# Dealing out statistics and residuals, and reordering three border tiles, in a three-pass decoder kernel

## The chip, the cores and the metric

The kernel runs on one core of a Trainium2 chip. The metric is the device time of one execution in microseconds (us). A core has five engines that run their own instruction streams and wait for each other by semaphores: TensorE (PE, matmuls), VectorE (DVE), ScalarE (ACT), GpSimd (POOL), and SyncE (SP), which starts the transfers here. Every stream is worked off in order.

## The reference, cut to what matters

x has 16 sequences of 256 tokens by 512 features. Three sublayers follow each other, each behind a layer norm and each added to x.

```
# 1 attention-like recurrence, R, K, V from time-mixed LN(x), 1024 wide
e  = exp(clip(W + K, -20, 10));  eu = exp(clip(U + K, -20, 10))
A  = shift(cumsum(e * V)) + eu * V;   B = shift(cumsum(e)) + eu
x  = x + (sigmoid(R) * A / B) @ Wo.T + bo
# 2 cross attention of LN(x) with ctx (one head as wide as the model)
s  = (Q @ K.T + side) / sqrt(32);  x = x + softmax(s) @ V @ Wo.T + bo
# 3 FFN on time-shifted LN(x), xr and xk
x  = x + sigmoid(xr @ Wr.T) * (relu(xk @ Wk.T)**2 @ Wv.T)
```

## The kernel before

Work is cut into 8 tiles of two sequences (512 tokens, four row blocks of 128 called s or SUB). Every matmul operand is split into a high and a low part, and a product is three matmuls (high·high, low·high, high·low; `three`, L80 to L82), so that a projection of one chunk is 12 matmuls of 512 columns. ACT writes most high parts; DVE or POOL subtracts to get the low ones (`..._rest`, `..._lo`). PSUM is used as eight banks: `bank[...]` for projections and turns (transposes on PE), `acc[s]` for the sublayer's output.

There are three passes over the tiles, each a block with a barrier at its end, and the result of a pass goes through memory to the next. Within a block the order of every engine's instructions is written out by hand.

**Attention pass.** `in_pairs` runs tile 0 alone, a hardware loop over the pairs (1,2), (3,4), (5,6), and tile 7 alone. A tile has eight chunks c of 128 output features, counted over tiles by g. For each chunk PE projects K, V and R (in this order), then the output of two chunks ago; in chunks 3 to 6 it also turns the next tile's normalised input. DVE's `body` (L736) does mix k, `quotient` and `refine` of the chunk before, `decayed` (L622), mix v, the two `clip`s (L628, L630), the scan, `weigh_own`, mix r, `weigh` (L646), the second scan and `denominator`. PE's V waits for weigh of the chunk before, and its K for decayed. ACT's body (L550) begins with `first_reciprocal` (L531) of the last chunk and ends with `log_d` (L526); the quotient on DVE needs both. The next tile's layer norm is made ahead: four `statistics` (L681) and an `aggregate` (L686) on DVE, `rstd_of` on POOL, four `normalise` (L474) on ACT. The previous tile's four `residual`s (L694) free its output banks.

**Cross pass.** `over_tiles(..., TAIL)` writes the first tile and the last two out alone, the others are a loop. In tile i PE makes scores, `query(i+1, c)`, `turn_probs`, `context(i, h)` and `output(i, c)` (L1137) with the turns of tile i+2 between. ACT makes `q_high`, `context_high` (L1209) of the next context, `probs_high` (L1232), `normalise(i+2)` (L1194), `pc_high` (L1236). DVE makes the low parts, POOL those of the context (`context_rest`, L1527) and rstd. In the last cross tile the FFN's first input is prepared too: `turn_ffn`, `leave_ffn`, `mix_ffn` (L1416) and its high and low parts, and PE ends with the receptance of row blocks 0 and 1.

**FFN pass.** Per tile: `receptance(i, s)`, `cap`, gate, `key(i, c)` with relu and square, the turns of tile i+1, `value`. In the first tile PE goes receptance 2 and 3, then keys with turns between them.

## Time and profile before

| | us |
|---|---|
| median of 3 runs | 1365.69 |
| their range | 1365.62 to 1366.47 |
| the profiled execution: time | 1365.3 |
| its span (first to last instruction) | 1363.3 |
| granted TensorE clock, mean | 0.997 of full speed |

Attention takes some 775 us of the span, cross attention 295, the FFN the rest. The profile is read in three steps: the busy times say which engine bounds; the waits say which stretches of that engine's idle time repeat, and who ended them; the timeline of a stretch shows each instruction with its start, its duration and, in brackets, the idle time of its engine before it with the event that ended it. PE's records overlap, since matmuls are pipelined: what a matmul costs is the distance of two starts, not its duration.

### The profile page before, as it was taken

To read this page: it belongs to the slowest core of one execution; us is meant where nothing else is said; L and a number is where in the kernel's file an instruction comes from. 1 tells how busy PE (TensorE), PEld (TensorE's weight loads), DVE (VectorE), ACT (ScalarE), POOL (GpSimd) and SP (SyncE) were. 2 spreads that over 40 slices of the span, in tenths; PEclk is the share of its full clock that TensorE was granted. 3 is DMA by queue.
4 is the path that set the end of the run, shared out by engine and by line. 5 is a ranking of instruction groups with operands and counts; after the bars stand their busy time and mean duration, and the time that the engine had idled before them with its cause. 6 is when DMAs were issued, how large, how long until landed. Compare 5 with 4: busy or idle time off the path is not lost. (4 is left out here: it accounts for less than half of the span.)

```text
span 1363.3 us, 19357 instructions
## 1 busy us (share of the span) xinstructions
PE 1324.1 (97%) x6330; PEld 1098.6 (81%) x6330; DVE 1096.6 (80%) x1782; ACT 817.8 (60%) x1555; POOL 632.7 (46%) x558
## 2 busy tenths in 40 slices
PE   6899999999999999999999989999999999999998
PEld 5777888887888888888887778888888778888886
DVE  6999999989999899999998766666554677777774
ACT  5875666666666666566556454444446366666664
POOL 4665344443443434434344554444446465555551
PEclk9999999999999999999999999999999999999999
DMA  9000101001001010010040454444442312222212
GB/s 351 10 28 5 62 32 57 7 31 62 25 6 62 31 62 0 31 62 0 32 193 1 177 224 159 154 144 148 143 162 110 123 32 93 92 92 92 93 62 93
DMA packets 54539, 113.92 MB, mean 84 GB/s; under 512 B 2768, under 2 KB 7120, under 8 KB 52560
## 3 DMA queue, kind: packets, MB, share of 16 engines
q1 hardware_dynamic: 54480, 113.22, 23.5%
q8 instruction: 26, 0.43, 0.1%
q14 instruction: 33, 0.27, 0.1%
HBM read 88.05 MB, written 25.17 MB: 83 GB/s over the span
## 5 line engine op out<-in xcount | busy, mean ns | idle before, releaser
L827 POOL TENSOR_TENSOR a_ss<-a_ss,a_eu 128x512 f32<-128x512 f32 x64 | 82.6, 1290 | 270.6 <-DVE a_ss L634 270.6
L494 ACT ACTIVATE k_or_row<-bank 128x512 f32<-128x512 f32 x192 | 114.9, 599 | 53.3 <-PE bank L82 49.2
L616 DVE SCALAR_TENSOR_TENSOR bank<-bank,k_or_row 128x510 f32<-128x510 f32 x192 | 132.1, 688 | 15.1 <-ACT k_or_row L494 10.2
L832 POOL TENSOR_TENSOR a_sv<-a_sv,a_euv 128x512 f32<-128x512 f32 x64 | 82.8, 1293 | 119.2 <-DVE a_sv L651 119.2
L514 ACT ACTIVATE bank<-bank,a_nbr 128x510 f32<-128x510 f32 x64 | 42.2, 659 | 119.3 <-DVE bank L616 119.3
L401 PE MATMUL bank<-a_wo_hi,a_y_hi 128*128 128x512 f32 x256 | 100.4, 392 | 0.0
L401 PE MATMUL bank<-a_wo_hi,a_y_lo 128*128 128x512 f32 x256 | 99.7, 389 | 0.0
L401 PE MATMUL bank<-a_wo_lo,a_y_hi 128*128 128x512 f32 x256 | 99.6, 389 | 0.0
L1532 POOL TENSOR_TENSOR b_cx_lo<-b_cx,b_cx_hi 128x512 fp32r<-128x512 f32 x32 | 40.6, 1297 | 112.8 <-ACT b_cx_hi L1214 112.8
L836 POOL TENSOR_TENSOR a_y_lo<-a_yy,a_y_hi 128x512 fp32r<-128x512 f32 x64 | 86.0, 1343 | 2.0 <-ACT a_y_hi L537 2.0
L634 DVE TENSOR_TENSOR_SCAN a_ss<-a_mask,a_ee 128x514 f32<-128x514 f32 x64 | 79.6, 1243 | 2.2
L651 DVE TENSOR_TENSOR_SCAN a_sv<-a_mask,a_ee 128x514 f32<-128x514 f32 x64 | 78.6, 1229 | 2.2
L1911 POOL TENSOR_TENSOR c_diff<-c_xt 128x512 f32<-128x512 f32 x28 | 35.5, 1267 | 80.9 <-ACT c_xt L1743 80.9
L509 ACT ACTIVATE a_ee<-a_ee,a_col 128x512 f32<-128x512 f32 x64 | 46.5, 726 | 36.6 <-DVE a_ee L622 36.6
L664 DVE TENSOR_TENSOR a_sv<-bank,a_sv 128x512 f32<-128x512 f32 x64 | 44.0, 687 | 25.8 <-ACT bank L531 25.7
L1236 ACT ACTIVATE b_pc_hi<-bank 128x512 fp32r<-128x512 f32 x32 | 19.1, 598 | 68.6 <-PE bank L82 68.6
L1916 POOL TENSOR_TENSOR c_mixed_k_lo<-c_mixed_k,c_mixed_k_hi 128x512 fp32r<-128x512 f32 x28 | 47.0, 1710 | 25.5 <-ACT c_mixed_k_hi L1749 25.5
L1326 DVE TENSOR_TENSOR b_pc_lo<-bank,b_pc_hi 128x512 fp32r<-128x512 f32 x32 | 22.1, 691 | 45.1 <-ACT b_pc_hi L1236 44.4
L1527 POOL TENSOR_TENSOR b_ct_lo<-b_ct,b_ct_hi 128x512 fp32r<-128x512 f32 x32 | 41.2, 1310 | 35.2 <-ACT b_ct_hi L1209 35.2
L401 PEld LDWEIGHTS bank<-a_wo_hi,a_y_hi 128*128 128x128 f32 x256 | 48.1, 188 | 10.4 <-issue 0.5
L401 PEld LDWEIGHTS bank<-a_wo_lo,a_y_hi 128*128 128x128 f32 x256 | 48.0, 188 | 10.4 <-issue 0.5
L401 PEld LDWEIGHTS bank<-a_wo_hi,a_y_lo 128*128 128x128 f32 x256 | 48.1, 188 | 10.0
(246 smaller groups left out, 4717.2 us busy)
## 6 DMA issues: line engine op xcount, KB each, us to landing
xres<-in_x SPq DMA_DIRECT2D x8, 1024.0 KB, 5.3
x_after_attention<-xres SPq DMA_DIRECT2D x8, 1024.0 KB, 4.3
xin<-x_after_attention SPq DMA_DIRECT2D x8, 1024.0 KB, 5.6
b_ct<-in_ctx_t SPq DMA_DIRECT2D x8, 1024.0 KB, 5.7
b_cx<-in_ctx SPq DMA_DIRECT2D x8, 1024.0 KB, 7.9
xres<-x_after_attention SPq DMA_DIRECT2D x8, 1024.0 KB, 5.5
x_after_cross<-xres SPq DMA_DIRECT2D x8, 1024.0 KB, 4.4
xin<-x_after_cross SPq DMA_DIRECT2D x8, 1024.0 KB, 5.6
```

Source lines behind the costliest of these rows:

```text
L401: last = te.matmul(acc[s][:, :], a[:, c % 2, t], b[:, c, :], start=(c == 0 and a is y_hi and b is wo_hi), stop=(c == HC - 1 and a is y_lo))
L494: sc.activation(u3[:, :, 1:], ps[m][:, :, :], ACT.Copy, scale=MIX[m]).then_inc(left[m], 1)
L509: sc.activation(ee3[:, :, 1:], ee3[:, :, 1:], ACT.Exp, bias=col[:, 1, c:c + 1]).then_inc(e_exp, 1)
L514: sc.activation(ps["r"][:, :, 0:T - 1], ps["r"][:, :, 0:T - 1], ACT.Exp, bias=nbr[:, c:c + 1], scale=-1.0).then_inc(r_exp, 1)
L616: ve.scalar_tensor_tensor(out=ps[m][:, :, 0:T - 1], in0=ps[m][:, :, 1:T], scalar=1.0 - MIX[m], in1=u3[:, :, 0:T - 1], op0=ALU.mult, op1=AL ...
L634: ve.tensor_tensor_scan(ss[:, :], mask_sb[:, :], ee[:, :], 0.0, ALU.mult, ALU.add).then_inc(s_scan, 1)
L651: ve.tensor_tensor_scan(sv[:, :], mask_sb[:, :], ee[:, :], 0.0, ALU.mult, ALU.add).then_inc(sv_scan, 1)
L664: ve.tensor_tensor(sv3[:, :, 0:T], work3[:, :, :], sv3[:, :, 0:T], ALU.mult).then_inc(q_done, 1)
L827: gp.tensor_tensor(ss3[:, :, 0:T], ss3[:, :, 0:T], eu[:, :, :], ALU.add).then_inc(b_done, 1)
L832: gp.tensor_tensor(sv3[:, :, 0:T], sv3[:, :, 0:T], euv[:, :, :], ALU.add).then_inc(a_done, 1)
L836: gp.tensor_tensor(y_lo[:, c % 2, :], flat(yy), y_hi[:, c % 2, :].bitcast(F32), ALU.subtract).then_inc(ylo_done, 1)
L1916: gp.tensor_tensor(m_lo[m][:, k, :], mixed_of(m, i)[:, k, :], m_hi[m][:, k, :].bitcast(F32), ALU.subtract).then_inc(mlo_done[m], 1)
```

## The change

Nothing is added or removed but positions, banks and the waits that go with them.

- Attention: DVE's statistics, aggregate and residuals, before in three bunches behind chunks 0 and 1, are dealt out over chunks 0 to 2 by a new function `between`. ACT's normalises, before a pair ahead of `exp_r` in chunks 1 and 2, are now a pair ahead of `exp_r` and a pair behind `log_d` in chunk 2. POOL's `rstd_of` goes from chunk 1 to 2.
- First cross tile: ACT does the probabilities first, then q_high(1,2), all four `context_high`, q_high(1,3), all four normalises; DVE and POOL in step.
- Last cross tile: `turn_ffn` 0 and 1 ahead of `turn_probs`, 2 and 3 behind the contexts, into the banks `acc[0]`, `acc[1]`, `bank[2]`, `bank[3]`; their leave, mix and high parts follow.
- First FFN tile: receptance(0,s) has bank s (`r_bank`); POOL's key rests come ahead of `rstd_of(1)`.

```diff
--- before.py
+++ after.py
@@ -567,9 +567,9 @@   (attention, ACT)
-                    if 1 <= c < 3 and ahead:
-                        normalise(i + 1, 2 * c - 2)
-                        normalise(i + 1, 2 * c - 1)
+                    if c == 2 and ahead:
+                        normalise(i + 1, 0)
+                        normalise(i + 1, 1)
                     exp_r(g, c)
...
                         log_d(g, 0)
+                    if c == 2 and ahead:
+                        normalise(i + 1, 2)
+                        normalise(i + 1, 3)
@@ -733,21 +736,36 @@   (attention, DVE)
+            def between(i, c):
+
+                if not is_last(i):
+                    if is_first(i) and 1 <= c < 3:
+                        statistics(1, 2 * c - 1)
+                    elif not is_first(i) and c < 2:
+                        statistics(i + 1, 2 * c)
+                    if c == 2:
+                        if is_first(i):
+                            dve.wait_ge(st_done, 2 * SUB)
+                        aggregate(i + 1)
+                if c == 2 and not is_first(i):
+                    residual(i - 1, (1,))
...
-                    if c == 1 and ahead:
+                    if c == 2 and ahead and not is_first(i):
                         dve.wait_ge(st_done, (i + 1) * SUB + SUB)
                     mix("k", g)
-                    if c == 1 and ahead:
-                        aggregate(i + 1)
+                    between(i, c)
                     if back:
                         quotient(g - 1)
                     decayed(g, c)
                     if back:
                         refine(g - 1)
+                    if c == 2 and not is_first(i):
+                        residual(i - 1, (2, 3))
                     mix("v", g)
...
-                    if c == 0 and ahead:
-                        for s in range(SUB):
-                            statistics(i + 1, s)
+                    if c < 2 and ahead:
+                        statistics(i + 1, 2 * c if is_first(i) else 2 * c + 1)
                     if c == 1 and not is_first(i):
-                        residual(i - 1, range(SUB))
+                        residual(i - 1, (0,))
@@ -856,7 +873,7 @@   (attention, POOL)
-                    if c == 1 and not is_last(i):
+                    if c == 2 and not is_last(i):
                         rstd_of(i + 1)
@@ -951,6 +968,10 @@   (cross)
+        def ffn_bank(k):
+
+            return acc[k] if k < 2 else bank[k]
@@ -1049,12 +1070,11 @@   (turn_ffn, PE)
                 if k < 2:
-                    pe.wait_ge(ptlo_done, NT * BT - 1 + k)
+                    pe.wait_ge(res_done, (NT - 1) * SUB)
                 else:
-                    pe.wait_ge(sh.k_mixed, k - 1)
+                    pe.wait_ge(ptlo_done, NT * BT - 3 + k)
@@ -1132,6 +1152,8 @@   (output, PE)
+                    if is_last(i):
+                        pe.wait_ge(sh.k_mixed, 2)
@@ -1161,6 +1183,9 @@   (body, PE)
+                else:
+                    turn_ffn(0)
+                    turn_ffn(1)
                 turn_probs(i, 0)
                 turn_probs(i, 1)
...
                 if is_last(i):
-                    turn_ffn(0)
-                    turn_ffn(1)
+                    turn_ffn(2)
+                    turn_ffn(3)
                 for c in range(KC):
-                    if is_last(i) and c in (1, 2):
-                        turn_ffn(c + 1)
                     output(i, c)
@@ -1279,8 +1302,6 @@   (body, ACT)
                     q_high(1, 1)
-                    for k in range(KC):
-                        context_high(1, k)
...
                 probs_high(i, 1)
-                if ahead:
+                if is_first(i):
+                    q_high(1, 2)
+                    for k in range(KC):
+                        context_high(1, k)
+                    q_high(1, 3)
+                    normalise(2, range(SUB))
+                elif ahead:
                     normalise(i + 2, (0, 1))
...
+                if not ahead:
+                    leave_ffn(0)
+                    leave_ffn(1)
                 for c in range(KC):
                     pc_high(i, c)
+                    if not ahead and c == 1:
+                        leave_ffn(2)
+                        leave_ffn(3)
                     if not ahead:
-                        leave_ffn(c)
-                        if c >= 2:
-                            mixed_high_ffn(c - 2)
+                        mixed_high_ffn(c)
@@ -1469,11 +1497,7 @@   (body, DVE)
                     q_rest(1, 0)
-                    statistics(2, (0, 1))
                     q_rest(1, 1)
-                    statistics(2, (2, 3))
-                    dve.wait_ge(st_done, 3 * SUB)
-                    aggregate()
...
+                if is_first(i):
+                    q_rest(1, 2)
+                    statistics(2)
+                    q_rest(1, 3)
+                    dve.wait_ge(st_done, 3 * SUB)
+                    aggregate()
...
+                if not ahead:
+                    mix_ffn(0)
+                    mix_ffn(1)
                 for c in range(KC):
+                    if not ahead and c >= 2:
+                        mixed_rest_ffn(c - 1)
                     pc_rest(i, c)
@@ -1557,7 +1591,11 @@   (body, POOL)
-                if not is_last(i):
+                if is_first(i):
+                    for k in range(KC):
+                        context_rest(1, k)
+                    rstd_of(2)
+                elif not is_last(i):
...
@@ -1626,6 +1664,10 @@   (FFN)
+        def r_bank(i, s):
+
+            return s if is_first(i) else s % 2
...
+                if isinstance(i, int) and i == 1 and k < 2:
+                    pe.wait_ge(capped, 3 + k)
...
-                if s >= 2:
+                if is_first(i):
+                    pass
+                elif s >= 2:
                     wait(pe, capped, i * SUB + s - 1)
...
+                elif is_first(i):
+                    pe.wait_ge(capped, 1 + c)
                 else:
                     wait(pe, capped, i * SUB + 3 + c)
...
-            rstd_of(1)
             for k in range(KC):
                 mixed_rest("k", 0, k)
+            rstd_of(1)
```

Three places of the engines' streams show what moved. The first is DVE in an even tile of the attention loop, from the end of chunk 1 into chunk 2: L657 (L660 after) is the denominator, L694 (L697) the residuals, L616 (L619) a mix, L664 and L665 the quotient, L622 (L625) decayed, L673 (L676) refine. Before:

```order
L657 SCALAR_TENSOR_TENSOR a_ss<-bank,a_ss 128x2x256
L694 TENSOR_TENSOR xres<-xres,bank 128x512 x4
L615 REGISTER_ALU
L616 SCALAR_TENSOR_TENSOR bank<-bank,k_or_row 128x2x255
L664 TENSOR_TENSOR a_sv<-bank,a_sv 128x2x256
L665 TENSOR_TENSOR bank<-bank,a_ss 128x512
L622 SCALAR_TENSOR_TENSOR a_ee<-a_trem,a_negw,bank 128x2x256
L673 SCALAR_TENSOR_TENSOR a_yy<-bank,a_sv 128x512
```

After:

```order
L660 SCALAR_TENSOR_TENSOR a_ss<-bank,a_ss 128x2x256
L684 BN_STATS stats<-xin 128x6
L697 TENSOR_TENSOR xres<-xres,bank 128x512
L759 ISA
L618 REGISTER_ALU
L619 SCALAR_TENSOR_TENSOR bank<-bank,k_or_row 128x2x255
L689 BN_AGGR mv<-stats 128x2 x4
L697 TENSOR_TENSOR xres<-xres,bank 128x512
L667 TENSOR_TENSOR a_sv<-bank,a_sv 128x2x256
L668 TENSOR_TENSOR bank<-bank,a_ss 128x512
L625 SCALAR_TENSOR_TENSOR a_ee<-a_trem,a_negw,bank 128x2x256
L676 SCALAR_TENSOR_TENSOR a_yy<-bank,a_sv 128x512
```

The fourth statistic and the aggregate have come in, and three of the four residuals stand inside chunk 2 (the last two follow directly behind these rows).

The second place is ACT in the first cross tile, behind q_high(1,1): L1209 (L1232 after) is context_high, L1232 (L1255) probs_high, L1194 (L1217) normalise, L1203 (L1226) q_high, L1236 (L1259) pc_high(0,0). Before:

```order
L1209 ACTIVATE b_ct_hi<-b_ct_5301 128x512 x4
L1232 ACTIVATE b_pt_hi<-bank2 128x512
L1232 ACTIVATE b_pt_hi<-bank3 128x512
L1194 ACTIVATE xin<-xin,nmr,rstd 128x512 x2
L1203 ACTIVATE b_q_hi_5303<-bank0,qb 128x512
L1194 ACTIVATE xin<-xin,nmr,rstd 128x512 x2
L1203 ACTIVATE b_q_hi_5303<-bank1,qb 128x512
L1236 ACTIVATE b_pc_hi<-bank0 128x512
```

After:

```order
L1255 ACTIVATE b_pt_hi<-bank2 128x512
L1255 ACTIVATE b_pt_hi<-bank3 128x512
L1226 ACTIVATE b_q_hi_5303<-bank0,qb 128x512
L1232 ACTIVATE b_ct_hi<-b_ct_5301 128x512 x4
L1226 ACTIVATE b_q_hi_5303<-bank1,qb 128x512
L1217 ACTIVATE xin<-xin,nmr,rstd 128x512 x4
L1259 ACTIVATE b_pc_hi<-bank0 128x512
```

The four context_high have moved behind the probabilities and one q_high, and all four normalises stand together ahead of pc_high.

The third place is POOL in the same tile: L1527 (L1561 after) is context_rest, the four rows from L1517 (L1551) the rstd chain. Before:

```order
L1527 TENSOR_TENSOR b_ct_lo<-b_ct,b_ct_hi 128x512 x2
L1517 TENSOR_TENSOR rstd<-mv,eps 128x4
L1518 TENSOR_SCALAR nmr<-mv 128x4
L1520 TENSOR_TENSOR rstd<-rstd,half 128x4
L1523 TENSOR_TENSOR nmr<-nmr,rstd 128x4
L1527 TENSOR_TENSOR b_ct_lo<-b_ct,b_ct_hi 128x512 x2
```

After:

```order
L1561 TENSOR_TENSOR b_ct_lo<-b_ct,b_ct_hi 128x512 x4
L1551 TENSOR_TENSOR rstd<-mv,eps 128x4
L1552 TENSOR_SCALAR nmr<-mv 128x4
L1554 TENSOR_TENSOR rstd<-rstd,half 128x4
L1557 TENSOR_TENSOR nmr<-nmr,rstd 128x4
```

The rstd chain, for which the normalises wait, now stands behind all four rests.

## Rows read from the trace of the kernel before

**Rows 1.** The page, first part: busy time of each engine.

```profile
PE 1324.1 (97%) x6330; PEld 1098.6 (81%) x6330; DVE 1096.6 (80%) x1782; ACT 817.8 (60%) x1555; POOL 632.7 (46%) x558
```

**Rows 2.** Waits of PE: us in total, times, longest.

```profile
PE bank L80 <- DVE a_ee L646: 6.6, 12, 1.1
```

**Rows 3.** Timeline, DVE, tile 0: start, us, engine, line, operation, operands, idle before.

```profile
35.52 0.74 DVE L622 SCALAR_TENSOR_TENSOR a_ee<-a_trem,a_negw,bank 128x512 f32<-128x512 f32 x1
...
60.38 1.52 DVE L630 TENSOR_SCALAR a_ee<-a_ee 128x512 f32<-128x512 f32 x1
```

**Rows 4.** Timeline, PE, tile 0, chunk 1's K.

```profile
36.40 0.47 PE L80 MATMUL bank<-a_xt_hi,a_wk_hi 128*128 128x512 f32 x1 [2.76 <-DVE a_ee L622]
```

**Rows 5.** Timeline, DVE, attention tile 2.

```profile
206.72 0.69 DVE L664 TENSOR_TENSOR a_sv<-bank,a_sv 128x512 f32<-128x512 f32 x1 [0.48 <-ACT bank L531]
...
215.46 2.46 DVE L681 BATCH_NORM_STATS2 stats<-xin 128x6 f32<-128x512 f32 x4
...
234.01 0.42 DVE L630 TENSOR_SCALAR a_ee<-a_ee 128x512 f32<-128x512 f32 x1
...
236.84 0.75 DVE L646 SCALAR_TENSOR_TENSOR a_ee<-bank,a_col,a_ee 128x512 f32<-128x512 f32 x1
...
240.80 0.69 DVE L664 TENSOR_TENSOR a_sv<-bank,a_sv 128x512 f32<-128x512 f32 x1 [0.76 <-ACT bank L531]
...
247.04 0.74 DVE L646 SCALAR_TENSOR_TENSOR a_ee<-bank,a_col,a_ee 128x512 f32<-128x512 f32 x1
```

**Rows 6.** Timeline, PE, attention tile 2: V of chunks 3 and 4.

```profile
237.64 0.50 PE L80 MATMUL bank<-a_xt_hi,a_wv_hi 128*128 128x512 f32 x1
...
249.15 0.39 PE L80 MATMUL bank<-a_xt_hi,a_wv_hi 128*128 128x512 f32 x1
```

**Rows 7.** Timeline, ACT, first cross tile.

```profile
804.65 2.18 ACT L1209 ACTIVATE b_ct_hi<-b_ct 128x512 fp32r<-128x512 f32 x4
...
814.42 0.60 ACT L1236 ACTIVATE b_pc_hi<-bank 128x512 fp32r<-128x512 f32 x1 [0.63 <-PE bank L82]
```

**Rows 8.** Timeline, POOL, first cross tile.

```profile
805.42 2.56 POOL L1527 TENSOR_TENSOR b_ct_lo<-b_ct,b_ct_hi 128x512 fp32r<-128x512 f32 x2 [12.62 <-ACT b_ct_hi L1209]
...
809.63 2.51 POOL L1527 TENSOR_TENSOR b_ct_lo<-b_ct,b_ct_hi 128x512 fp32r<-128x512 f32 x2
```

**Rows 9.** Timeline, PE, first cross tile.

```profile
812.73 0.36 PE L80 MATMUL bank<-b_pt_hi,b_cx_hi 128*128 128x256 f32 x1 [2.35 <-DVE b_q_lo L1334]
...
816.14 0.39 PE L1137 MATMUL bank<-b_l_hi,b_pc_hi 128*128 128x512 f32 x1
```

**Rows 10.** Timeline, PE, last cross tile.

```profile
1057.89 0.58 PE L80 MATMUL bank<-b_pt_hi,b_cx_hi 128*128 128x256 f32 x1 [1.41 <-DVE b_pt_lo L1326]
...
1063.12 0.48 PE L1137 MATMUL bank<-b_l_hi,b_pc_hi 128*128 128x512 f32 x1
...
1065.94 0.28 PE L80 MATMUL bank<-b_pt_hi,b_cx_hi 128*128 128x256 f32 x1
...
1078.99 0.50 PE L80 MATMUL bank<-c_wr_hi,c_mixed_r_hi 128*128 128x512 f32 x1 [0.24 <-DVE c_mixed_r_lo L1428]
```

**Rows 11.** Stretches: us; busy (x) PE, PEld, DVE, ACT, POOL; granted clock; DMA.

```profile
37.20:41.40 4.20, 3.78 (x10) 2.51 (x9) 4.13 (x8) 4.12 (x9) 1.28 (x1) 0.59 0.00 0
1058.00:1062.40 4.40, 4.40 (x25) 4.40 (x26) 0.69 (x1) 0.60 (x1) 4.40 (x5) 0.63 0.47 184
```

**Rows 12.** Timeline, ACT, first FFN tile.

```profile
1091.13 2.94 ACT L1736 ACTIVATE xin<-xin,nmr,rstd 128x512 f32<-128x512 f32 x4 [1.69 <-POOL nmr L1903]
```

**Rows 13.** Timeline, PE, first FFN tile.

```profile
1085.80 0.50 PE L80 MATMUL bank<-c_wr_hi,c_mixed_r_hi 128*128 128x512 f32 x1 [1.07 <-DVE c_gate L1828]
...
1092.48 0.47 PE L80 MATMUL bank<-c_mixed_k_hi,c_wk_hi 128*128 128x512 f32 x1 [0.90 <-POOL c_mixed_k_lo L1916]
...
1106.89 0.48 PE L1705 MATMUL bank<-c_wv_hi,c_k_hi 128*128 128x512 f32 x1
```

**Rows 14.** Timeline, POOL, first FFN tile.

```profile
1091.06 5.01 POOL L1916 TENSOR_TENSOR c_mixed_k_lo<-c_diff,c_mixed_k_hi 128x512 fp32r<-128x512 f32 x4
```

31 lines of the change are left out of this document (13 added, 18 removed).

## The prediction

> **What bounds the kernel now.** The page's first part comes first: PE is busy for 1324.1 of a span of 1363.3 us [rows 1], so a reordering can win or lose only in PE's idle stretches. The waits of PE show the largest repeated ones [rows 2]: 12 of the attention pass for DVE's weighted V, 6.6 us in all and none above 1.1. The timelines then place these and the single ones. Each stretch that the change touches is read apart: attention tile 0, a later attention tile, the first cross tile, the last cross tile, the first FFN tile.
>
> **Part A, attention.** No instruction is added; four statistics, the aggregate, four residuals and four normalises per tile change place. DVE's order decides when PE may start the next V projection (behind weigh, L646) and K projection (behind decayed, L622).
>
> Tile 0: four statistics in a row take 2.46, as in tile 2 [rows 5], and stand ahead of chunk 1's decayed at 35.52, behind which PE waits 2.76, its longest wait in the tile [rows 3, 4]. After the change one stands behind chunk 0 and one behind mix k, so two of four, 1.2 us, leave that place, and the quotient ahead has less to wait for: decayed comes some 1.5 earlier and the wait shrinks to about 1.3. But the second pair of normalises now stands between chunk 2's logarithm and its reciprocal on ACT, 1.47 (half of four at 2.94 [rows 12]), in the chain log, reciprocal, quotient, decayed. By adding up the engine orders, chunk 2's chain ends only .15 before its old place: most of the gain is lent, and new waits of V take it back. I take −1.0; bounds 0 (all given back) and −2.8 (all of the 2.76 kept).
>
> In the same tile a clip of DVE took 1.52 [rows 3], where the same instruction takes .42 in tile 2 [rows 5]; POOL was splitting weight rows at the time. If DVE's row slides out of that coincidence, 1.1 is won there, if it slides into another it is lost; this is inside the bounds. The Trainium skill ("SBUF — State Buffer", section "Who interferes with whom") calls the port pair that VectorE and GpSimd share an exclusive lock, so that the engine which issues second stands still: by it the extra 1.1 is a matter of which of the two comes first, and tile 0 would come out at about −.15 or −1.25 instead of −1.0. The trace agrees as far as 1.52 against .42 goes, and doesn't tell which comes first after the change.
>
> Tile 1: its three late V projections lie behind the same bunch of statistics and residuals; −.5, an estimate at half of one long wait of 1.1 [rows 2].
>
> Tiles 2, 4, 6: DVE waits .48 for ACT ahead of a quotient in chunk 0 [rows 5]; one statistic (.62, a quarter of 2.46 [rows 5]) moved ahead of it fills that hole. All other moved steps still stand between this point and chunk 2's weigh. So weigh (.75 at 236.84 [rows 5]) comes about .5 earlier, some .1 of it by the wait for the input that is no longer late, and PE's V of chunk 3 (237.64 [rows 6]) is bound .3 to .4 earlier: −.4 each. What is late next is chunk 3: the pair of normalises, 1.47 less about .7 that the chain has gained ahead of it, moves the quotient at 240.80, which already waits .76 for ACT, so chunk 3's weigh (.74 at 247.04 [rows 5]) ends near 248.55, against V of chunk 4 at 249.15 − .4 = 248.75 [rows 6]. The slack is about .2, so it is hidden, barely.
>
> Tiles 3, 5 begin behind the loop's edge, where DVE starts late and has no hole to fill. The same work stands ahead of weigh; the normalise pair costs about +.1 each. Tile 7 has nothing to prepare.
>
> Sum of A: −1.0 − .5 − 1.2 + .2 = −2.5 (0 to −4.3).
>
> **Part B, first cross tile.** ACT did context_high of tile 1 (2.18 at 804.65), probabilities, normalises, and pc_high(0,0) at 814.42 [rows 7]; POOL two context rests (2.56), the rstd chain, two more (2.51 at 809.63) [rows 8]; PE waited 2.35, began context(0,0) at 812.73, and output(0,0) at 816.14 [rows 9].
> After the change the probabilities go first. PE's context(0,0) then needs no longer wait till 812.73; it starts near 810.15. But ACT's four context_high stand behind q_high(1,2), and that behind PE's query(1,2): two turns of probabilities (some .9) and 12 matmuls (2.8, as in the output of [rows 10]) behind query(1,1), which ACT had taken over before 804.65. I reckon its end at 807.6, so q_high ends at 808.2 and context_high at 810.3. POOL starts its four rests .77 behind the first of them, as it did before (805.42 against 804.65), at 808.95, and needs 2.56 + 2.51 less an overlap: 813.95. The rstd chain is now behind all four: from the end of the first pair at 807.98 to 809.63 it took 1.65, with a start lag 1.75, so 815.7. ACT's four normalises wait for it and take 2.85 (2.94 [rows 12] less overlap): 818.55. Only behind these stands pc_high(0,0): .60 and DVE's rest .75 make output(0,0) possible at 819.95. **That is 3.85 later than 816.14.** PE has done contexts (0,0) and (0,1) (1.4 each and a .7 wait between) by about 813.7, and idles some 6.2.
>
> The clock comes on top. PE fell idle for 2.76 before 36.40 [rows 4], and the stretch from 37.20 shows a granted clock of .59 over 4.20 us; after two waits of 1.41, the second of them at 1057.89 [rows 10], the stretch from 1058.00 shows .63 over 4.40 [rows 11]: 1.7 and 1.6 us lost, at the lower level of 1.2 GHz for most of each. After the 2.35 at 812.73 no fall shows. An idle of 6.2 is far beyond all three: +1.6 (0 to 2.3, the upper bound if the lower level lasts a third longer). The Trainium skill ("TensorE: Matmul & The Clock Gate", section "What's actually happening") says that the throttled state is the default and that activity releases it; by it a stretch at 1.2 GHz would surely follow this idle, and the lower bound 0 would fall away.
>
> Sum of B: +5.45 (+3.85 to +6.15).
>
> **Part C, last cross tile.** Before, PE made turns of the FFN input behind context and between the outputs. From output(0) at 1063.12 to the receptance at 1078.99 it took 15.87 [rows 10]. One output took 2.82, to 1065.94 [rows 10]; four are 11.0 where no turn slows their first matmul, and two contexts of half as many columns 2.8; the other 2.1 are two turns and waits. After: turns 0 and 1 fill the idle of 1.41 ahead of 1057.89 [rows 10], 2 and 3 follow the contexts. context(0) stays at 1057.89, since its probabilities bind. Two mix_ffn (three DVE instructions of about .69 each, the length of those in [rows 5]; 4.15) fit from 1057.75 to 1061.9, then the pc rest, and output(0) starts at 1062.7 to 1063.2 with all turns done. Plus 13.8: receptance at 1076.5 to 1077.0. **−2.2** (−2.5 at best; −1.5 if the pc rest comes one .7 step later than that).
>
> **Part D, first FFN tile.** Block entry is T = 1085.20; receptance(0,2) waited till 1085.80, key(0,0) began at 1092.48 with a wait for POOL, value at 1106.89, T + 21.69 [rows 13]. After: receptance starts at T (−.6), and POOL's four rests (5.01 [rows 14]) come first, done at T + 5.45 when key(0,0) wants them, so its four waits (2.3 in all) go. But rstd_of(1) is now behind them: T + 7.15, normalises 2.94 [rows 12], T + 10.3, and turn(1,0), which stands behind key(0,0) (T + 8.15) on PE, idles 2.2. Keys 2 and 3 wait .65 more for ACT, which is late by the normalises. Value at T + 20.9: −.8 (0 to −2.8; the latter if ACT had the normalises free in time).
>
> **Sum:** −2.5 + 5.45 − 2.2 − .8 = −.05. The profiled run had 1365.3 with a span of 1363.3; the median is 1365.69. On the median: **1365.6**, no change that a measurement can tell (it tells about 0.2%, 2.7 us, so 1363.0 to 1368.4 is "same").
>
> **Rivals.**
> *1. Faster: the new wait in the first cross tile doesn't come.* If the statistics reach POOL or the ct rests leave it sooner than I add up, pc_high isn't held and output(0,0) starts near 813.7: −2.4 in place of +5.45, so 1357.8. Against it: the orders put rstd behind four POOL rests and pc_high behind four normalises, on in-order engines. .08.
> *2. Faster: tile 0 and the FFN keep what they gain.* A to −4.0, D to −2.3: 3 us less, 1362.6. For it: the 2.76 and the four key waits are real; against: the normalise chains that follow. .16.
> *3. Slower: ACT's normalise pair, in the chain between logarithm and reciprocal.* It decides once chunk 3's chain is later than the .2 of slack. If it comes .85 later, chunk 4's V of six loop tiles starts .6 later than in the forecast: +3.6, A = +1.1, 1369.2. For it: 1.47 stands in a chain with .2 of slack; against: the earlier weigh gives part back. .12.
> *4. Slower: the dealt-out work only changes place (A = 0)*, 1368.1, and with the long clock stretch 1368.8: .10, half of it above 1368.4.
> *5. The change doesn't do what it says in the FFN:* ACT's normalises bind and D is 0: 1366.4, within "same".
> The forecast with 5 holds .54. Range 1360.5 to 1369.5: below lies rival 1, above the ends of 3 and 4. Faster .24 (1 and 2), same .54, slower .22 (3, part of 4, and sums of bounds in B).
>
> **What the profile of the changed kernel would show.** B: the gap before output(0,0) near 6 us, released by DVE's pc rest or ACT, normalises in front of pc_high, and a clock of about .6 behind it; if that gap is below 2, B is wrong. A: the wait before tile 0's second K at about 1.3, V waits of tiles 2, 4, 6 below .1 at chunk 3, and no new ones at chunk 4. C: the receptance some 13.8 behind output(0). D: no wait for the key rests, one of about 2 at turn(1,0) behind normalise. The forecast falls if loop tiles differ by over .5 each, since there are six of them.

## The result, and the profile after

The changed kernel takes 1368.97 us (median of 18 runs), the kernel before 1366.22 in the same runs (18): ratio 1.0021, 95% interval 1.0015 to 1.0027, so **2.75 us slower**. The profiled execution of the changed kernel has a span of 1365.2 against 1363.3.

Where the time went is read best from landmarks on PE, at which the work left to do is the same in both: the first matmul of a tile's last attention output, of a cross tile's first output, of the FFN's receptance, of a tile's first value. A stretch's difference is its length between two landmarks after, less before.

| stretch (up to) | before, at | after, at | difference | forecast |
|---|---|---|---|---|
| first projection | 15.60 | 15.23 | −.36 | (no part of the change) |
| attention tile 0 | 129.91 | 128.61 | −.93 | −1.0 |
| tile 1 | 221.03 | 218.98 | −.75 | −.5 |
| tiles 2, 4, 6 | | | −.12, −.19, −.33 | −.4 each |
| tiles 3, 5 | | | +.33, +.46 | +.1 each |
| tile 7, to the first scores | 789.47 | 787.58 | 0 | 0 |
| first cross output | 816.14 | 817.97 | +3.72 | +3.85 |
| second tile's output | 852.51 | 855.81 | +1.47 | +1.6 |
| last cross tile's first output | 1063.12 | 1065.97 | −.45 | −.2 |
| receptance of the FFN | 1078.99 | 1079.89 | −1.95 | −2.0 |
| first value | 1106.89 | 1108.73 | **+.94** | **−.8** |
| end | | | +.02 | 0 |

The sum is +1.86. Two lines are off: the FFN's, which has the wrong sign, and the attention loop's odd tiles. (The last cross tile's forecast of −2.2 is split here at its first output, by its own working.) A landmark stands one chunk into the next tile, since an output comes two chunks behind its projections; so an even tile's stretch includes the beginning of the odd tile behind it.

The waits of PE after (line, who ended them: us in total, times, longest):

```profile
PE bank L80 <- DVE a_ee L649: 8.8, 11, 2.0
PE bank L1159 <- DVE b_pc_lo L1354: 6.8, 2, 6.1
PE bank L1713 <- ACT xin L1784: 2.9, 1, 2.9
...
PE bank L80 <- DVE a_ee L625: 1.2, 1, 1.2
```

Against [rows 2] the attention's waits for the weighted V (L649 now) have grown from 6.6 to 8.8, and three new waits have come, one in each reordered border tile: 6.06 in the first cross tile, .73 in the last (the other of the two in the second line) and 2.88 in the first FFN tile. Tile 0's wait for decayed has shrunk from 2.76 [rows 4] to 1.2.

First cross tile, timelines of ACT, POOL and PE, and the stretch behind the first output (us, busy of PE, PEld, DVE, ACT, POOL, granted clock, DMA):

```profile
808.40 0.69 ACT L1226 ACTIVATE b_q_hi<-bank,qb 128x512 fp32r<-128x512 f32 x1
813.79 2.93 ACT L1217 ACTIVATE xin<-xin,nmr,rstd 128x512 f32<-128x512 f32 x4 [4.70 <-POOL nmr L1557]
816.62 1.05 ACT L1259 ACTIVATE b_pc_hi<-bank 128x512 fp32r<-128x512 f32 x2
```

```profile
807.02 5.04 POOL L1561 TENSOR_TENSOR b_ct_lo<-b_ct,b_ct_hi 128x512 fp32r<-128x512 f32 x4 [16.12 <-ACT b_ct_hi L1232]
812.00 0.22 POOL L1551 TENSOR_TENSOR rstd<-mv,eps 128x4 f32<-128x4 f32 x1
```

```profile
810.24 0.38 PE L80 MATMUL bank<-b_pt_hi,b_cx_hi 128*128 128x256 f32 x1 [0.46 <-DVE b_q_lo L1362]
817.97 0.79 PE L1159 MATMUL bank<-b_l_hi,b_pc_hi 128*128 128x512 f32 x1 [6.06 <-DVE b_pc_lo L1354]
```

```profile
817.90:822.00 4.10, 4.03 (x12) 3.23 (x13) 3.59 (x10) 0.00 (x0) 0.75 (x1) 0.64 0.00 0
1097.00:1101.50 4.50, 4.38 (x14) 3.64 (x15) 1.38 (x2) 4.40 (x9) 0.00 (x0) 0.62 0.00 0
```

This is the chain of the prediction, event by event: POOL's four rests to 812.0, the rstd chain, ACT's four normalises at 813.79 after 4.70 of idle, and only then both pc_high. PE waits 6.06, and the granted clock is .64 over the 4.1 us behind. In [rows 9] there was an idle of 2.35 here, and in [rows 7] pc_high stood behind two pairs of normalises that were done in time. The second line of the last fence is the FFN's: there too the granted clock is .62 over 4.5 us, and that was not in the forecast.

First FFN tile, timelines of PE, POOL and ACT:

```profile
1085.82 0.47 PE L80 MATMUL bank<-c_wr_hi,c_mixed_r_hi 128*128 128x512 f32 x1 [0.32 <-PEq L918]
...
1091.36 0.39 PE L80 MATMUL bank<-c_mixed_k_hi,c_wk_hi 128*128 128x512 f32 x1
...
1097.12 0.98 PE L1713 MATMUL bank<-ident_sb,xin 128*128 128x128 f32 x4 [2.88 <-ACT xin L1784]
```

```profile
1086.51 5.05 POOL L1964 TENSOR_TENSOR c_mixed_k_lo<-c_diff,c_mixed_k_hi 128x512 fp32r<-128x512 f32 x4 [11.41 <-ACT c_mixed_k_hi L1797]
1091.51 0.67 POOL L1945 TENSOR_TENSOR rstd<-mv,eps 128x4 f32<-128x4 f32 x1
...
1092.33 1.43 POOL L1948 TENSOR_TENSOR rstd<-rstd,half 128x4 f32<-128x4 f32 x1
```

```profile
1094.14 2.93 ACT L1784 ACTIVATE xin<-xin,nmr,rstd 128x512 f32<-128x512 f32 x4 [3.92 <-POOL nmr L1951]
```

Receptance and key start without the waits of [rows 13], as forecast: the key 5.54 behind the block's entry. But the first turn waits 2.88 for the normalises, which wait for POOL's rstd chain.

Last cross tile: one move of this part does not stand in the diff above. POOL's memset of the margin (`sh.margin`, for which every `mix_ffn` waits) stood behind POOL's twelve weight rests, and stands ahead of them now. Before, the first mix waited for it; after, it doesn't, and comes 7.9 earlier counted from the first output of the tile before (1034.26, after 1037.65). POOL and DVE before, then DVE after:

```profile
1065.44 0.10 POOL L1576 MEMSET c_xt<- 128x8 f32 x1
1065.63 0.70 DVE L1416 TENSOR_TENSOR bank<-bank,c_xt 128x512 f32<-128x512 f32 x1 [0.85 <-POOL c_xt L1576]
```

```profile
1061.14 0.69 DVE L1444 TENSOR_TENSOR bank<-bank,c_xt 128x512 f32<-128x512 f32 x1
```

The early mix of part C needs this move as much as the early turns; no run takes it out alone, so its share of the gain is open.

An even attention tile (tile 2), ACT and DVE around the end of chunk 2:

```profile
236.98 0.60 ACT L526 ACTIVATE bank<-a_ss 128x512 f32<-128x512 f32 x1 [0.53 <-DVE a_ss L660]
237.52 1.51 ACT L474 ACTIVATE xin<-xin,a_nmr,rstd 128x512 f32<-128x512 f32 x2
238.93 0.63 ACT L531 ACTIVATE bank<-bank,a_shift 128x512 f32<-128x512 f32 x1
```

```profile
239.59 0.69 DVE L667 TENSOR_TENSOR a_sv<-bank,a_sv 128x512 f32<-128x512 f32 x1 [2.05 <-ACT bank L531]
```

The pair of normalises stands between logarithm (L526) and reciprocal (L531), and DVE's quotient waits 2.05 for it, where it waited .76 [rows 5]: 1.29 lost to DVE in each of tiles 1 to 6. Whether PE feels it is the question of the experiments.

The odd tile that follows (tile 3): DVE's last residuals and PE's output of chunk 0 in chunk 2, and PE's V of chunk 3, before and after.

```profile
320.02 1.27 DVE L697 TENSOR_TENSOR xres<-xres,bank 128x512 f32<-128x512 f32 x2
```

```profile
320.30 0.39 PE L401 MATMUL bank<-a_wo_hi,a_y_lo 128*128 128x512 f32 x1
320.75 0.50 PE L401 MATMUL bank<-a_wo_hi,a_y_hi 128*128 128x512 f32 x1
```

```profile
327.73 0.50 PE L80 MATMUL bank<-a_xu_hi,a_wv_hi 128*128 128x512 f32 x1 [0.53 <-DVE a_ee L646]
325.78 0.50 PE L80 MATMUL bank<-a_xu_hi,a_wv_hi 128*128 128x512 f32 x1 [0.61 <-DVE a_ee L649]
```

The V wait was there before, and has grown by .08 only. More is lost at the output: its third bank is free when the third residual is done (the first of the pair at 320.02, which ends near 320.7), and PE starts on it .45 behind the matmul before, where the others start .23 apart. PE's lead on the kernel before shrinks by .34 there.

### The profile page after: what moved, and what is told of

The parts are those of the page before. It is cut to its first block and busy times, and to the rows that moved or that the text cites. A ratio compares the mean times of both kernels' runs of the same rounds, so it can differ in the third digit from the quotient of the medians.

```text
span 1365.2 us, 19356 instructions
## 1 busy us (share of the span) xinstructions
PE 1322.3 (97%) x6330; PEld 1098.1 (80%) x6330; DVE 1095.9 (80%) x1782; ACT 814.9 (60%) x1555; POOL 634.9 (47%) x558
## 5 line engine op out<-in xcount | busy, mean ns | idle before, releaser
L619 DVE SCALAR_TENSOR_TENSOR bank<-bank,k_or_row 128x510 f32<-128x510 f32 x192 | 132.3, 689 | 7.0 <-issue 4.0
L1259 ACT ACTIVATE b_pc_hi<-bank 128x512 fp32r<-128x512 f32 x32 | 19.0, 596 | 68.2 <-PE bank L82 68.2
L1561 POOL TENSOR_TENSOR b_ct_lo<-b_ct,b_ct_hi 128x512 fp32r<-128x512 f32 x32 | 41.1, 1308 | 38.7 <-ACT b_ct_hi L1232 38.7
L1159 PE MATMUL bank<-b_l_hi,b_pc_hi 128*128 128x512 f32 x128 | 52.5, 410 | 6.8 <-DVE b_pc_lo L1354 6.8
L526 ACT ACTIVATE bank<-a_ss 128x512 f32<-128x512 f32 x64 | 38.5, 601 | 32.4 <-DVE a_ss L660 32.4
```

The lines of the kernel that those rows point to most:

```text
L619: ve.scalar_tensor_tensor(out=ps[m][:, :, 0:T - 1], in0=ps[m][:, :, 1:T], scalar=1.0 - MIX[m], in1=u3[:, :, 0:T - 1], op0=ALU.mult, op1=AL ...
```

## The experiments

All times are medians; "against before" is the difference to the median of the kernel before in the same group of runs (1366.56 for the first four, 1366.47 for the next four, 1366.80 for the last four). The changed kernel stands at +2.75. The ratio in brackets counts all executions, also the few long ones of the last section, so in runs 5 and 8, which have several, it lies above the ratio of the medians. A difference to the changed kernel joins four medians, and by the spread of the times it is uncertain by some .9 either way; so the differences of 1.0 or less in runs 2, 5 and 11 are not clear of noise by the times alone, and are read from landmarks. These repeat well: from receptance to first value all six profiles with the FFN tile as changed have +.91 to +.94 against before, and both with the old one (runs 2 and 7) −.15. Unless it says otherwise an experiment is the changed kernel with one edit.

**1. The first cross tile put back.**

```diff
@@ (cross, ACT; DVE and POOL likewise) @@
+                    for k in range(KC):
+                        context_high(1, k)
...
-                if is_first(i):
-                    q_high(1, 2)
...
-                    normalise(2, range(SUB))
-                elif ahead:
+                if ahead:
                     normalise(i + 2, (0, 1))
```

> The changed kernel with the first cross tile put back into its old order on ScalarE, VectorE and GpSimd; everything else changed. Theory (the new wait of 6.1 us ahead of the first output, and the half clock behind it, are a loss that nothing gives back): about 5.1 less than the changed kernel, 1363.9 where that has 1369.0, so some 2.3 below the kernel before. Rival (the engines that run ahead during the wait give it back in the next cross tiles, and the loss sits in the loop tiles or the FFN): within 1 us of the changed kernel, 1368 to 1369.

Measured: 1364.24, −2.3 against before (ratio 0.9986, interval 0.9977 to 0.9995), 5.1 less than the changed kernel. The loss of this tile is real and is not given back later, and without it the kernel is faster than the one before: all other parts together gain 2.3. (In this run's profile the clock fell behind the old order's wait of 2.34, which it did not behind the 2.35 before; its first output comes .93 later than there.)

**2. The first FFN tile put back** (banks, waits, and rstd ahead of the rests).

```diff
-            return s if is_first(i) else s % 2
+            return s % 2
...
+            rstd_of(1)
             for k in range(KC):
                 mixed_rest("k", 0, k)
-            rstd_of(1)
```

> The changed kernel with the first FFN tile put back (banks, waits, and GpSimd's rstd ahead of the key rests). Theory from the two profiles (the new order of this tile loses .9: it takes away five waits of some 3.5 us, but adds one of 2.9 at the first turn and a stretch of half clock of some 1.7 behind it): .9 less than the changed kernel, 1368.1. Rival (the new order gains .8 as forecast, and the loss is elsewhere): .8 more, 1369.8.

Measured: 1368.31, +1.75 against before (1.0018, 1.0008 to 1.0029), 1.0 less than the changed kernel. The new order of this tile loses, as the profiles say and the forecast did not: by landmarks 1.1 (−.15 here, +.94 in the changed kernel).

**3. Both pairs of normalises ahead of the sigmoid exponential.**

```diff
                     if c == 2 and ahead:
-                        normalise(i + 1, 0)
-                        normalise(i + 1, 1)
+                        for s in range(SUB):
+                            normalise(i + 1, s)
...
-                    if c == 2 and ahead:
-                        normalise(i + 1, 2)
-                        normalise(i + 1, 3)
```

> The changed kernel with the second pair of normalises of the attention pass ahead of chunk 2's sigmoid exponential, together with the first, instead of between its logarithm and the reciprocal. Theory (the pair in that chain sets DVE back by 1.28 us from chunk 3 on in every tile; at the tile's end DVE is still .7 behind what PE has gained, and the odd tiles, which start from there, lose .5): the setback shrinks to some .6, the waits of PE for weigh in chunk 3 of tiles 3 and 5 from .78 to about .4, tiles 1 to 6 gain .2 to .4 each, 1367.5 (1366.8 to 1368.2) where the changed kernel has 1369.0. Rival (the odd tiles lose because the statistics stand ahead of their first quotient, behind the 2.05 of loop edge): no change, 1368.7 to 1369.3, and the waits stay at .78.

Measured: 1368.07, +1.5 against before (1.0012, 1.0003 to 1.0021), 1.25 less than the changed kernel. By landmarks, tiles 2 to 6 change from −.12, +.33, −.19, +.46, −.33 to −.43, −.30, −.47, −.06, −.45, that is 1.86 us gained, while tile 0 loses its .93: there PE now waits for the denominator of chunk 2, behind the four normalises (1.02). The odd tiles' share in the gain (.63 and .52) is there. But the waits at chunk 3 of tiles 3 and 5 shrink only from .61 and .66 to .52 and .56, and were .53 before the change, so they are not where most of the loss sat (the expectation's .78 counts the same wait from start to start). What is gone is the stop at the output of chunk 0: PE's lead on the kernel before, which shrank by .34 and .32 there in tiles 3 and 5, no longer shrinks. The loop edge is unchanged and can't be the cause by itself.

**4. The first cross tile's normalises later**, and nothing else moved.

```diff
                     q_high(1, 3)
-                    normalise(2, range(SUB))
...
                     pc_high(i, c)
+                    if is_first(i) and c == 1:
+                        normalise(2, range(SUB))
```

> The changed kernel with ScalarE's four normalises of the first cross tile behind the second high part of the context (pc_high) instead of ahead of the first; nothing else is moved. Theory (these four, which wait for GpSimd's rstd chain, are what holds the first output up): the output starts near 811.7 + 1.5 instead of 817.97 in the profile, the half clock behind it goes, and the next wait is below 1 us at the first turn of tile 2: about 6.5 less than the changed kernel, 1362.5. Rival (the rests of the context on GpSimd or VectorE's own queue hold it): the wait of 6.1 stays, or moves unshrunk to the turn, 1368 to 1369.

Measured: 1361.49, −5.1 against before (0.9964, 0.9951 to 0.9978), 7.8 less than the changed kernel. Its timeline of PE, and the stretch behind the first output:

```profile
811.87 0.38 PE L80 MATMUL bank<-b_pt_hi,b_cx_hi 128*128 128x256 f32 x1 [0.46 <-DVE b_q_lo L1363]
...
813.38 0.40 PE L1159 MATMUL bank<-b_l_hi,b_pc_hi 128*128 128x512 f32 x1
```

```profile
813.30:817.40 4.10, 4.10 (x26) 3.59 (x25) 1.68 (x4) 2.56 (x4) 3.96 (x7) 1.00 0.87 317
```

The wait of 6.06 is gone, not shrunk, and the granted clock is 1.00. The place of these four instructions alone held the tile; the rest of the tile's new order is a gain: to the first output this tile is now 2.4 shorter than before, of which .9 go again up to the next tile's output, where the first turn waits .7 for the normalises.

**5. The first FFN tile's normalises and turns put off.**

```diff
-                    if s == 1 and not is_last(i):
+                    if s == 1 and not is_last(i) and not is_first(i):
                         normalise(i + 1)
                 for c in range(KC):
                     relu_square(i, c)
+                    if is_first(i) and c == 0:
+                        normalise(1)
...
+                    if is_first(i):
+                        if c == 2:
+                            turn(1, 0)
+                        if c == 3:
+                            for k in (1, 2, 3):
+                                turn(1, k)
```

> The changed kernel with the first FFN tile's next steps put off: ScalarE makes tile 1's four normalises behind the first key's relu and square instead of ahead of gates 2 and 3, and TensorE turns tile 1's input behind keys 2 and 3 instead of one turn behind each key. Theory (the first FFN tile loses because the turn behind the first key waits 2.9 us for normalises that wait for GpSimd's rstd, now late, and the clock halves behind that wait): the wait of 2.9 and the half clock go, the remaining waits together stay near 1 us, the value begins some 18.9 behind the block's entry where the changed kernel has 22.9, that is 4 us less, 1365 where the changed kernel has 1369.0. Rival (ScalarE's whole chain of gates and relus binds this tile, so that the wait only moves to the third key): at most 1.5 less, 1367.5 to 1369.

Measured: 1368.67, +2.2 against before (1.0024, 1.0012 to 1.0036), only .55 less than the changed kernel (.87 by landmarks, up to the second tile's value). The wait of 2.88 and the low clock behind it are gone, and the value begins 20.5 behind the block's entry instead of 22.9 (1.53 less than before from receptance to value), though one turn ahead of it still waits 1.49 for ACT. The next tile then gives 1.60 back; its receptance now waits for a low part of mixed_r, which comes late by the turns. The rival is nearer: in this tile ACT has no room, and what PE is spared comes back at the next thing that ACT makes.

**6. The loop's normalises where ACT idles**: one behind y_high, three ahead of the sigmoid exponential; tile 0 as changed.

```diff
                         y_high(g - 1, (c - 1) % HC)
+                    if c == 2 and ahead and not is_first(i):
+                        normalise(i + 1, 0)
...
+                    elif c == 2 and ahead:
+                        for s in (1, 2, 3):
+                            normalise(i + 1, s)
...
-                    if c == 2 and ahead:
+                    if c == 2 and ahead and is_first(i):
                         normalise(i + 1, 2)
                         normalise(i + 1, 3)
```

> The changed kernel with ScalarE's normalises of tiles 1 to 6 placed in chunk 2 where ScalarE idles: one behind y_high, three ahead of the sigmoid exponential; none is left between logarithm and reciprocal. Tile 0 stays as changed. Theory (the pair in that chain was the loss of the odd tiles): tiles 1 to 6 together change from +.3 (tiles 2 to 6: -.1, +.3, -.2 to +.1, +.5, -.3, tile 1 -.75) to about -2.5 against the kernel before, so 1.9 less than the changed kernel, 1367.1, and DVE's setback at chunk 3 is below .2. Rival (loop edge): 1369.0.

Measured: 1366.86, +.4 against before (1.0008, 0.9998 to 1.0018), 2.35 less than the changed kernel. ACT and DVE in tile 2 of this run:

```profile
231.15 0.80 ACT L474 ACTIVATE xin<-xin,a_nmr,rstd 128x512 f32<-128x512 f32 x1
...
233.15 2.21 ACT L474 ACTIVATE xin<-xin,a_nmr,rstd 128x512 f32<-128x512 f32 x3
...
238.07 0.60 ACT L526 ACTIVATE bank<-a_ss 128x512 f32<-128x512 f32 x1 [0.54 <-DVE a_ss L665]
238.71 0.66 ACT L531 ACTIVATE bank<-bank,a_shift 128x512 f32<-128x512 f32 x1
```

```profile
239.40 0.69 DVE L672 TENSOR_TENSOR a_sv<-bank,a_sv 128x512 f32<-128x512 f32 x1 [0.76 <-ACT bank L531]
```

The quotient waits .76 again, as before the change. Tiles 1 to 6 by landmarks: −.82, −.43, −.29, −.45, −.15, −.45, in sum −2.6. The same statistics and residuals, dealt out as in the changed kernel, no longer lose in the odd tiles: it was the pair in the chain. The gain of the odd tiles is less firm than the end of their loss: with the same edit tiles 3 and 5 have −.08 and +.11 in run 8, −.23 and −.19 in run 9, where all eight profiles with the pair in the chain have +.32 to +.35 and +.46 to +.51.

**7. The last cross tile alone**: the kernel before with this part of the change only (the hunks on `turn_ffn`, `ffn_bank`, leave, mix and rests of the last cross tile in the diff above, and POOL's early memset).

> The kernel before with only the last cross tile's part of the change. Theory (this part stands by itself, two turns and two short waits leave the path behind the first output): 2.4 to 2.5 less than the kernel before, 1363.9 where that has 1366.4. Rival (it gains only because the loss in the first cross tile has let the other engines run ahead): 0 to 1 less, 1365.4 to 1366.4.

Measured: 1364.15, −2.3 against before (0.9987, 0.9975 to 0.9999). The part stands by itself; by landmarks it is −2.4 from the second cross tile's output to the receptance.

**8. Experiments 4, 5 and 6 together.**

> The changed kernel with three things mended: the first cross tile's normalises behind the second pc_high, the loop tiles' normalises in ScalarE's idle places, the first FFN tile's normalises and turns late. Theory (the losses stand in three separate stretches, so their removal adds up): 7.5 + 1.9 + 4 less than the changed kernel, 1355.6 (1354.5 to 1357.5), which is also below the kernel before by 10. Rival (part of what is won early is given back at the next late engine): 1358 to 1361.

Measured: 1358.88, −7.6 against before (0.9962, 0.9947 to 0.9977). The three measured gains, 7.8 + .55 + 2.35, taken from +2.75 give −7.95: they add up, by medians. (4 of the 12 executions are long here, and the ratio, which counts them, says −5.2.) The expected 1355.6 had the FFN's 4 us in it, which run 5 denies.

**9. Run 8 with pauses for GpSimd in the last cross tile.**

```diff
                 pool.wait_ge(fwhi_done, n + 1)
+                if n == 9:
+                    pool.wait_ge(sh.r_rest, 1)
...
                 for s in range(SUB):
+                    if is_last(i) and s % 2 == 0:
+                        pool.wait_ge(sh.r_rest, 2 + s // 2)
```

> The run e8_all_mended with three added waits of GpSimd in the last cross tile: ahead of its tenth weight rest for VectorE's first low part of mixed_r, and ahead of the first and third bias addition for the second and third. Theory (some executions of every kernel with the new last cross tile are 6 to 7 us longer, because VectorE's two-operand subtraction waits for a port as long as GpSimd goes on without a gap; one profile shows 8.81 us for it where the others have 1.4): the four subtractions take .68 each in the profile and no execution lies more than 3 us above the median, where 4 of 12 of e8_all_mended did; the median falls by .3 to .7, to 1358.3. Rival (the long executions have another cause): again 2 to 4 of 12 are 6 us longer.

Measured: 1358.51, −8.3 against before (0.9937, 0.9924 to 0.9950), 5 runs from 1357.78 to 1359.36. None is long; with 5 runs, and a share of 4 in 12 in run 8, that is not yet proof. Of the four subtractions two take .68 and two 1.8 and 1.7, so the pauses free two of them, where four were expected. With run 8, from which its median can't be told apart, this is the fastest version, and beats both kernels.

**10. GpSimd's rstd chain of the first cross tile back between the pairs of rests.**

```diff
-                    for k in range(KC):
-                        context_rest(1, k)
+                    context_rest(1, 0)
+                    context_rest(1, 1)
                     rstd_of(2)
+                    context_rest(1, 2)
+                    context_rest(1, 3)
```

> The changed kernel with GpSimd's rstd chain of the first cross tile between its two pairs of context rests, as before the change; ScalarE and VectorE stay as changed. Theory (the wait of 6.06 is ScalarE's place for the four normalises, and GpSimd's new place for rstd has a share in it): VectorE's aggregate ends at 810.47 in the changed kernel's profile and rstd starts at 812.00, so that chain, the normalises and the first output come 1.5 earlier: the wait falls to 4.5, the half clock behind it stays, 1.5 less than the changed kernel, 1367.5. Rival (GpSimd's order is the whole cause): the wait falls to 2 or less and the half clock goes, 1363.

Measured: 1367.75, +.95 against before (1.0012, 1.0002 to 1.0022), 1.8 less than the changed kernel. PE, and the stretch behind:

```profile
817.74 0.79 PE L1159 MATMUL bank<-b_l_hi,b_pc_hi 128*128 128x512 f32 x1 [4.59 <-DVE b_pc_lo L1354]
```

```profile
817.70:822.70 5.00, 4.96 (x12) 3.90 (x13) 4.61 (x8) 0.00 (x0) 4.09 (x3) 0.51 0.44 180
```

4.59 where 4.5 was expected, with a clock of .51 behind it. So of the 6.06, POOL's place for rstd is 1.5, and ACT's place for the normalises all of it, since run 4 takes the whole away with POOL unchanged. In time the profile has less: the lower clock lasts longer into the outputs here (some 2.4 us lost against 1.5 in the changed kernel), and up to the second tile's output only .56 of the 1.5 is left. The median's 1.8 has more in it than this profile shows.

**11. The FFN's banks without GpSimd's new order.**

```diff
+            rstd_of(1)
             for k in range(KC):
                 mixed_rest("k", 0, k)
-            rstd_of(1)
```

> The changed kernel with GpSimd's rstd chain of the first FFN tile back ahead of the key rests; the new banks and their waits stay. Theory (the banks let the receptance start .6 sooner, but the key waits for the same rests as before, so they bring nothing by themselves, and the new place of rstd is the whole loss): the turn no longer waits, the four waits for the key rests return with some 3 us in all, the value starts 21.7 behind the block's entry, 1.0 less than the changed kernel, 1368.0. Rival (the banks keep their gain): 1.6 less or more, 1367.4 or lower.

Measured: 1368.93, +2.1 against before (1.0014, 1.0005 to 1.0022), .6 less than the changed kernel, where 1.0 was expected. From the receptance to the first value it is still .57 longer than before. PE and the clock:

```profile
1095.85 0.47 PE L80 MATMUL bank<-c_mixed_k_hi,c_wk_hi 128*128 128x512 f32 x1 [1.71 <-POOL c_mixed_k_lo L1964]
```

```profile
1098.00:1101.50 3.50, 3.36 (x12) 2.43 (x12) 1.50 (x2) 3.08 (x6) 1.45 (x2) 0.56 0.00 0
```

The banks bring the receptance forward by .6 to .7, and the key then waits 1.71 where it waited .90 [rows 13]; behind this one longer wait the clock falls to .56, which it did not behind the shorter ones before. The waits of the tile are shorter in sum (2.4 where they were 2.7), and yet it takes longer. So I was wrong to expect that rstd's new place is the whole loss: the banks have their share, by a clock that halves.

**12. The FFN's turns put off, ACT as changed.**

```diff
                     key(i, c)
-                    if not is_last(i):
+                    if is_first(i):
+                        if c == 2:
+                            turn(1, 0)
...
+                    elif not is_last(i):
                         turn(i + 1, c)
```

> The changed kernel with TensorE's turns of tile 1 in the first FFN tile behind keys 2 and 3; ScalarE keeps its normalises ahead of gates 2 and 3. Theory (behind the normalises ScalarE's gates and the first relu bind, 15.2 behind the block's entry, and key 2 needs that relu): the wait of 2.9 only moves from the turn to key 2, where it is about 4, the half clock stays, and the tile is 0 to 1 us longer than in the changed kernel: 1369 to 1370. Rival (the turn's place is the cause of the loss): 2 to 3 less, 1366 to 1367.

Measured: 1375.88, +9.1 against before (1.0066, 1.0053 to 1.0079), 6.3 more than the changed kernel, where 0 to 1 was expected. PE's new wait in this tile:

```profile
PE bank L80 <- ACT c_ka L1820: 6.4, 2, 4.0
```

The wait moves to the third key, 4.0 long as expected, and a second one of 2.35 that I had not reckoned with stands at the fourth: ACT's next relu stands behind a leave, which waits for the turn that was put off. In this tile ACT's chain is what binds.

## Why the prediction was wrong, point by point

The time lies in the range (1368.97, with 1369.5 as its upper end), but the forecast was no change and the measured one is +2.75. That it lies in the range is luck: the upper end came from rival 3's 1369.2, and V of chunk 4 late in six loop tiles, from which that was worked out, did not come. By landmarks the parts are A −1.5 (forecast −2.5), B +5.2 (+5.45), C −2.4 (−2.2) and D +.94 (−.8): the errors of D and A, 1.7 and 1.0, are the miss.

- **Part B, first cross tile: right.** Step by step the chain came as worked out; +5.2 by landmarks (3.72 and 1.47) against +5.45, and run 1 measures 5.1. Rival 1 is dead: the wait was there. That an idle of 6 us would bring the lower clock was right, .64 behind it. ("After the 2.35 at 812.73 no fall shows" holds for that profile alone: runs 1 and 7 have the same code, and the fall.) Runs 4 and 10 show that the normalises' place holds the output and that POOL's place of rstd makes 1.5 of it.
- **Part C, last cross tile: right.** −2.4 by landmarks and −2.3 by itself in run 7, against −2.2. The receptance is 13.9 behind the first output (1065.97 to 1079.89), 13.8 were forecast. The forecast put the two early mixes at 1057.75 without naming what they wait for; POOL's memset is moved too, so they could start.
- **Part D, first FFN tile: wrong sign, +.94 instead of −.8.** The term that failed is "turn(1,0) idles 2.2". It had two faults. The rstd chain was taken at 1.65 from the cross tile; here it took 2.6, its first step .67 instead of .21, the power 1.43 instead of 1.05, so that the wait became 2.88. Beside it VectorE's two-operand step of the gate (L1887) took 1.72, where it takes .69 in run 11, whose rstd chain comes elsewhere and takes 1.04 for the power; that the two hold each other up is likely, not shown. And the clock: I had priced a low-clock stretch for part B from [rows 11] and put it at nothing, without a reason, behind a wait of 2.2 in part D. The profile shows a granted clock of .62 over 4.5 us there, some 1.7 us lost (.38 of 4.5); the five other profiles with this wait have the fall too. The two faults, .7 and 1.7, less the .65 of waits at keys 2 and 3 that I had added and that did not come, make the error of 1.75. (The 2.3 of the four key waits is counted from start to start; as idle time it is 1.7.) Run 2 measures the part at 1.0 (1.1 by landmarks), and run 11 shows that the banks hold .4 of it (.7 by landmarks).
- **Part A: tiles 0 and 1 right in size, the loop short.** Tile 0's wait shrank to 1.16 at K as forecast (1.3), and new waits of V came (2.02). In runs 1, 2, 4 to 6, 10 and 12 the clock halved there and the tile still gained .8: PE waits for DVE in the next chunk anyway, so the low clock there costs next to nothing. DVE's slow clip did slide out of its coincidence: 1.52 at 60.38 became .43, and one a chunk earlier went from 1.42 to .42. So some of the .93 may be chance and not the dealt-out work; neither the −.15 nor the −1.25 that the text worked out for the two cases came.
- **The odd tiles: +.4 each instead of +.1, the even ones −.2 instead of −.4.** The step that failed is "The slack is about .2, so it is hidden, barely". It asked only whether chunk 4's V would be late in the same tile. It isn't, and at chunk 3's V the even tiles have their .4, as forecast. But the 1.29 that the pair takes from DVE is won back only slowly; at the end of tile 2 the last denominator comes at 291.77 instead of 293.42, 1.65 earlier, where PE's last R projection comes 2.34 earlier (283.62 instead of 285.96). The odd tile begins from DVE's place (first mix at 294.49 instead of 296.21, 1.72 earlier), and there PE gives back what it had gained, in three places: .15 at V of chunk 1, which still counts to the even tile; .34 at the output of chunk 0, which waits for a residual; and some .26 at V of chunks 3 and 4 (against .24 won at V of chunk 2). The second is the largest, and no term of the forecast stands for it: the change put the last three residuals into chunk 2, and what PE's next output waits for was not asked. Rival 3 had named the pair and the place, but as a V that is late in the same tile. Runs 3 and 6 take the pair out of the chain, the residuals stay where the change put them, and the loss of the odd tiles is gone; so the pair is the cause, and the late residual is how most of it reaches PE.

The two profiles account for +1.86 of the measured 2.75, of which the start's −.36 is no part of the change. The profiled execution of the changed kernel, 1367.07, is also the shortest of its 18; the kernel before was profiled at 1365.3, .9 below its median, and this one 1.9 below. Two stretches differ from execution to execution: PE's first projection starts at 15.23 here, the earliest of the 14 profiles (15.39 to 16.48 in the others, 15.60 before), and from the first cross output to the next tile's the low clock costs +1.47 here, the least of seven profiles with that wait (up to 2.41). Against the means of the other profiles (16.04 and 1.83) that is .4 each, if the early start of the kernel before is taken off; it would make up most of the missing .9, as an estimate. A low-clock stretch in tile 0, as in run 4, is not enough: it costs the tile .1.

## What to carry to other kernels

An instruction that an in-order engine makes for a later tile has to stand behind everything that the current tile waits for; the same four normalises cost a wait of 6 us ahead of two short casts and one of .7 behind them. A chain's slack is not spent where it is spent: follow the late engine to the end of the tile and into the next one, for there it stands late against an engine that has gained. Work that frees a buffer is waited for as well: where residuals are put off, ask which output needs their banks. Every wait that one adds or lengthens gets the question whether the clock falls behind it; merging short waits into a longer one can lose time although their sum shrinks, as in run 11.
